# Routing weights packed by token parity: spreads on 64 rows of the array, bias on 128 rows

## What is computed

```
a = layer_norm(channel_norm(x)) * w + b
left  = mask * (a @ Wl + bl) * sigmoid(a @ Gl + gl);  right likewise
t[i,j,c] = sum_k left[i,k,c] * right[j,k,c]              # one 256x256x256 product per channel
x = x + (layer_norm(t) @ Wo + bo) * sigmoid(a @ Wg + bg)
y = layer_norm(x)
p = softmax(y @ Wr + br)                                  # 8 experts
top-2 of p, renormalised to g1 + g2 = 1
x = x + sum over the 2 picked experts e of g_e * (y @ We[e] + be[e])
```

## Time and profile before

| | |
|---|---|
| median of 3 runs | 1189.2 us (1185.09 to 1192.96) |
| profiled execution | 1190.0 us, of it the span in the profile 1188.0 us |
| PE busy | 1080.7 us (91%) |
| PEld busy | 594.6 us (50%) |
| DVE busy | 882.2 us (74%) |
| POOL busy | 747.6 us (63%) |
| ACT busy | 598.8 us (50%) |

### The profile page before, as it was taken

One profiled execution on the slowest core, in us unless ns is written; L12 is line 12 of the kernel. 1 busy time (PEld: TensorE's weight loads), 2 busy tenths in 40 slices (PEclk: granted clock), 3 DMA queues, 4 the chain that ended last, 5 costly groups with the idle time before them and its releaser, 6 DMA issues.

```text
span 1188.0 us, 21300 instructions
## 1 busy us (share of the span) xinstructions
PE 1080.7 (91%) x5402; PEld 594.6 (50%) x5402; DVE 882.2 (74%) x3030; ACT 598.8 (50%) x1070; POOL 747.6 (63%) x728
## 2 busy tenths in 40 slices
PE   1788989889786599999999999999999999999987
PEld 1566666678674344444444444444444444454432
DVE  3999999611115768888888888887888788888872
ACT  0455666411111245666566556565656565656552
POOL 5777888121222357777777767776767776777632
PEclk9899999899887879999999999999999999999986
DMA  7388679967770101111111111111111111111100
GB/s 194 115 268 284 229 274 293 328 198 235 209 234 27 30 19 51 46 45 42 50 47 44 36 54 40 49 45 45 36 53 36 54 36 53 36 54 36 36 27 27
DMA packets 98895, 119.15 MB, mean 100 GB/s; under 512 B 6390, under 2 KB 72182, under 8 KB 96758
## 3 DMA queue, kind: packets, MB, share of 16 engines
q1 hardware_dynamic: 97138, 117.74, 30.9%
q10 hardware_dynamic: 1668, 0.46, 0.2%
HBM read 67.33 MB, written 50.33 MB: 99 GB/s over the span
## 4 chain that ended last, share of the span: by engine, by line
PE 75%; DVE 14%; issue 5%; DMA 2%; ACTq 1%; POOL 1%; ACT 1%; SPq 1%; DVEq 0%; POOLq 0%
PE b_m L807 22%; PE ring L793 9%; PE ein L710 7%; DVE stage L889 6%; PE b_d L754 6%; PE b_g L746 6%; PE b_t L747 5%; PE pr_a L672 4%; PE b_m L801 3%; DVE bst L876 3%; PE b_g L741 3%; PE b_g L735 3%; PE ring L815 3%; PE b_t L735 2%; PE ring L822 1%
## 5 line engine op out<-in xcount | busy, mean ns | idle before, releaser
L451 POOL TENSOR_TENSOR zb<-bcs,x2d 128x512 f32<-128x512 f32 x224 | 285.7, 1275 | 234.8 <-ACT bcs L588 233.6
L807 PE MATMUL b_m<-zb,w_exp 128*64 128x512 f32 x1024 | 284.7, 636 | 0.1
L1052 DVE TENSOR_TENSOR zb<-ring,x2d 128x512 f32<-128x512 f32 x288 | 197.5, 686 | 90.9 <-PE ring L793 90.2
L588 ACT ACTIVATE bcs<-ring 128x512 f32<-128x512 f32 x224 | 133.9, 598 | 245.5 <-PE ring L793 245.2
L572 ACT ACTIVATE x2d<-x2t 64x512 f32<-64x512 f32 x256 | 160.5, 627 | 3.4
L672 PE MATMUL pr_a<-w_proj,xts 64*128 64x256 f32 x1024 | 138.3, 399 | 22.1 <-DVE stage L889 21.4
L889 DVE SCALAR_TENSOR_TENSOR stage<-pr_a,mt,sig_a 128x128 f32<-128x128 f32 x512 | 147.8, 418 | 9.4 <-ACT sig_a L521 9.4
L793 PEld LDWEIGHTS ring<-wt,sel 32*128 32x128 f32 x512 | 49.4, 186 | 177.6 <-DVE zb L1052 83.1
L793 PE MATMUL ring<-wt,sel 32*128 32x512 f32 x512 | 131.0, 504 | 5.2 <-DVE zb L1052 4.4
L672 PEld LDWEIGHTS pr_a<-w_proj,xts 64*128 64x128 f32 x1024 | 95.1, 189 | 51.0 <-issue 30.9
L521 ACT ACTIVATE sig_a<-pr_a 128x512 f32<-128x512 f32 x128 | 76.4, 597 | 78.9 <-PE pr_a L672 78.9
(11 more groups left out here) (133 smaller groups left out, 1820.7 us busy)
## 6 DMA issues: line engine op xcount, KB each, us to landing
left_right_scratch<-stage SPq DMA_DIRECT2D x16, 2048.0 KB, 7.5
chunk<-left_right_scratch SPq DMA_DIRECT2D x24, 1024.0 KB, 9.0
xc<-in_x SPq DMA_DIRECT2D x64, 256.0 KB, 2.7
out<-outc SPq DMA_DIRECT2D x64, 256.0 KB, 2.0
chunk<-left_right_scratch SPq DMA_DIRECT2D x12, 384.0 KB, 7.5
chunk<-left_right_scratch SPq DMA_DIRECT2D x8, 192.0 KB, 4.9
chunk<-left_right_scratch SPq DMA_DIRECT2D x4, 256.0 KB, 8.0
chunk<-left_right_scratch SPq DMA_DIRECT2D x8, 64.0 KB, 4.7
```

What stands on the lines that cost most here:

```text
L451: pool.tensor_tensor(zb[:, m % NZ, :], bcs[:, tiles_before(POOL_TILES, ku, ku, m) % 2, :], x2d[:, ku % 2, m % 2, :], ALU.mult)\
L588: act.activation(bcs[:, tiles_before(POOL_TILES, ku, ku, m) % 2, :], ring[:, bcast_bank(ku % 2, m), :], ACT.Copy).then_inc(bcast_out, 1)
L807: ins = pe.matmul(b_m[t * C:(t + 1) * C, :], w_exp[:, ep, :], zb[:, (2 * ep + t) % NZ, :], start=False, stop=ep == EP - 1, skip_group_chec ...
L1052: dve.tensor_tensor(zb[:, m % NZ, :], ring[:, bcast_bank(ku % 2, m), :], x2d[:, ku % 2, m % 2, :], ALU.mult)\
```

## The change

- In a step, the token order becomes `(j t h)`: on the 128 rows of one transpose, rows 0 to 63 now hold the tokens of parity 0, the even unit's on the first 32 and the odd unit's on the second 32, and rows 64 to 127 those of parity 1. It is made by the two VectorE instructions that put the logits and the variances into that order.
- A spread of parity `m % 2` now reads the 64 rows `64*(m%2)` onward. Since those rows hold both units, `sel` has a second form (`sel[:, w]`, `w` the unit's parity) whose rows of the other unit are zero.
- The bias matmuls now read all 128 rows, with `bias_hi` and `bias_lo` in two forms in the same way.
- Set-up: `eb_wide`, `bias_hi`, `bias_lo` and `sel` are twice as wide; GpSimd makes `sel` with two instructions of 128x512, and one of 128x16 and a wait are gone.

```diff
-            ("sel", [P, E, C], F32R), ("kind", [P, 4, E]),
+            ("sel", [P, 2, E, C], F32R), ("kind", [P, 4, E]),
...
-                    sp.dma_start(eb_wide[row:row + E, t % 2 * C:t % 2 * C + C], expert_b).then_inc(const_in, 16)
+                    sp.dma_start(eb_wide[row:row + E, t % 2, t // 2 * C:t // 2 * C + C], expert_b).then_inc(const_in, 16)
...
-            pool.tensor_tensor(kind[:, 0:2, :], kind[:, 0:2, :], kind[:, 2:4, :], ALU.add).then_inc(sel_made, 1)
-            pool.wait_ge(sel_made, 2)
-            ins = pool.tensor_tensor(sel[:, :, :], kind[:, 0, :].unsqueeze(2).broadcast_to([P, E, C]),
-                                     kind[:, 1, :].unsqueeze(2).broadcast_to([P, E, C]), ALU.add)
+            for w in range(2):
+                ins = pool.tensor_tensor(sel[:, w, :, :], kind[:, w, :].unsqueeze(2).broadcast_to([P, E, C]),
+                                         kind[:, 2 + w, :].unsqueeze(2).broadcast_to([P, E, C]), ALU.add)
...
-                rows = slice(ku % 2 * 2 * ROUTE + m % 2 * ROUTE, ku % 2 * 2 * ROUTE + m % 2 * ROUTE + ROUTE)
-                pe.matmul(ring[:, bcast_bank(ku % 2, m), :], sel[rows, m // 2 * 2:m // 2 * 2 + 2, :].rearrange("p e c -> p (e c)"),
+                rows = slice(m % 2 * 2 * ROUTE, (m % 2 + 1) * 2 * ROUTE)
+                pe.matmul(ring[:, bcast_bank(ku % 2, m), :], sel[rows, ku % 2, m // 2 * 2:m // 2 * 2 + 2, :].rearrange("p e c -> p (e c)"),
                           wt[rows, ku // 2 % 2, :], start=True, stop=True).then_inc(bcast_ready, 1)
...
-                rows = slice(ku % 2 * 2 * ROUTE, (ku % 2 + 1) * 2 * ROUTE)
                 for part, b in enumerate((bias_hi, bias_lo)):
-                    pe.matmul(b_m[:, :], b[rows, :], wt[rows, ku // 2 % 2, :], start=part == 0, stop=False, skip_group_check=True)
+                    pe.matmul(b_m[:, :], b[:, ku % 2, :], wt[:, ku // 2 % 2, :], start=part == 0, stop=False, skip_group_check=True)
...
-            dve.tensor_copy(bias_hi[:, :], eb_wide[:, :]).then_inc(set_step, 1)
+            dve.tensor_copy(bias_hi[:, :, :], eb_wide[:, :, :]).then_inc(set_step, 1)
...
-                            ins = dve.tensor_scalar(v32[:, 0:TOK].rearrange("p (j h t) -> p h j t", h=2, t=2), x_stat[:, :, :, 2].rearrange("p (h j) t -> p h j t", h=2), 1.0 / C, EPS_LN, ALU.mult, ALU.add)
+                            ins = dve.tensor_scalar(v32[:, 0:TOK].rearrange("p (j t h) -> p h j t", h=2, t=2), x_stat[:, :, :, 2].rearrange("p (h j) t -> p h j t", h=2), 1.0 / C, EPS_LN, ALU.mult, ALU.add)
...
-                dve.tensor_copy(lg[:, b, :, :].rearrange("p (z j h t) e -> p z j h (t e)", z=2, j=2, h=2)[:, :, :, h, :],
-                                logits).then_inc(back_done, 1)
+                dve.tensor_copy(lg[:, b, :, :].rearrange("p (z j t h) e -> p z j t h e", z=2, j=2, h=2)[:, :, :, :, h, :],
+                                logits.rearrange("p z j (t e) -> p z j t e", t=2)).then_inc(back_done, 1)
```

More of the change, by code:

```diff
@@ L127, in metaformer_kernel @@
         w_og = keep("w_og", [P, 2, P])
-        bias_hi = keep("bias_hi", [P, P], F32R)
-        bias_lo = keep("bias_lo", [P, P], F32R)
+        bias_hi = keep("bias_hi", [P, 2, P], F32R)
+        bias_lo = keep("bias_lo", [P, 2, P], F32R)
         router_bias = keep("router_bias", [P, E])
@@ L147, in metaformer_kernel @@
             ("w_nat", [C, 6, 2, C]), ("ln_col", [P, 4]), ("bias_row", [1, 6 * C]), ("w_diff", [P, 6 * C]),
-            ("ones", [P, P]), ("e_nat", [P, E, C]), ("r_nat", [P, E]), ("eb_wide", [P, P]),
+            ("ones", [P, P]), ("e_nat", [P, E, C]), ("r_nat", [P, E]), ("eb_wide", [P, 2, P]),
             ("mask_in", [P, 2, N])])
-        setup_bytes = 4 * (12 * C + 4 + 6 * C + 6 * C + P + E * C + E + P + 2 * N)
+        setup_bytes = 4 * (12 * C + 4 + 6 * C + 6 * C + P + E * C + E + 2 * P + 2 * N)
         (xts, _, w_proj, mt, r_all, b_all, xa, xs, sig_a, stage, bst, nv, nh, ny, nt) = layer([
@@ L329, in _ @@
             pool.memset(w_router, 0.0).then_inc(pool_const, 1)
-            pool.memset(eb_wide[:, :], 0.0).then_inc(pool_const, 1)
+            pool.memset(eb_wide[:, :, :], 0.0).then_inc(pool_const, 1)
             pool.memset(w_og[:, :, :], 0.0).then_inc(pool_const, 1)
@@ L790, in bcast @@
                     if isinstance(u, int) and u == 0:
-                        pe.wait_ge(sel_made, 3)
-                rows = slice(ku % 2 * 2 * ROUTE + m % 2 * ROUTE, ku % 2 * 2 * ROUTE + m % 2 * ROUTE + ROUTE)
-                pe.matmul(ring[:, bcast_bank(ku % 2, m), :], sel[rows, m // 2 * 2:m // 2 * 2 + 2, :].rearrange("p e c -> p (e c)"),
+                        pe.wait_ge(sel_made, 2)
+                rows = slice(m % 2 * 2 * ROUTE, (m % 2 + 1) * 2 * ROUTE)
+                pe.matmul(ring[:, bcast_bank(ku % 2, m), :], sel[rows, ku % 2, m // 2 * 2:m // 2 * 2 + 2, :].rearrange("p e c -> p (e c)"),
                           wt[rows, ku // 2 % 2, :], start=True, stop=True).then_inc(bcast_ready, 1)
@@ L929, in _ @@
                 dve.tensor_tensor(w_router[part, half * E:half * E + E], r_nat[part, :], ps_set[part, 7, 0:E], ALU.subtract)
-            dve.tensor_copy(bias_hi[:, :], eb_wide[:, :]).then_inc(set_step, 1)
+            dve.tensor_copy(bias_hi[:, :, :], eb_wide[:, :, :]).then_inc(set_step, 1)
             dve.wait_ge(set_step, 2)
-            dve.tensor_tensor(bias_lo[:, :], eb_wide[:, :], bias_hi[:, :].bitcast(F32), ALU.subtract).then_inc(set_dve, 1)
+            dve.tensor_tensor(bias_lo[:, :, :], eb_wide[:, :, :], bias_hi[:, :, :].bitcast(F32), ALU.subtract).then_inc(set_dve, 1)
             with dve.Fori(0, CHUNKS) as c:
```

## The result

The changed kernel takes 1169.86 us (median of 3 runs, 1169.37 to 1174.58) against 1189.2: 19.3 us less, and the ratio of the means of the runs is 0.985 with a 95% interval of 0.9818 to 0.9883. That is faster by over 1%, which had a chance of 0.39. The direction was right; of the size, the forecast had 11 of the 19 us. The profiled execution took 1169.4 us (span 1167.4), to be held against 1190.0 before.

What follows compares the result with a forecast made beforehand. TensorE's own list was taken to bound the unit stage. From 1190.0 us, 12.3 came off for the bias pair and 0.3 was added for copies and the narrow gap, giving 1178.0 us, range 1171 to 1189.

Steps and rivals of the forecast that it cites:

- What bounds the kernel: Unit stage: TensorE's own list is the time, busy 696.57 of 705.00 us, as long as VectorE keeps up.
- The opening cost after a change of shape: Bias pair behind transposes: no shape change on 128 rows saves 0.215 us in 57 units, 12.3 us less.
- an fp32r record is one run, 0.213 us: Bias pair: two runs of 512 columns take 0.43 us, leaving 0.23 of its 0.66 for the shape change.
- Spreads on 64 rows at no cost: 256 spread pairs on 64-row halves run side by side as before: 0, with ends of 0 and 1.0 us more.
- The halves overlap: Spread pairs; judges the slower rival that 64-row fp32r matmuls don't run side by side: 1233 us, chance 0.06.
- VectorE's cover: VectorE copies cost 0, covered by 62.3 us of waits for spreads; smallest typical gap 0.30 us falls to 0.08.
- Set-up: Before the unit stage: extra GpSimd work is hidden behind 6.06 us of idle time until TensorE's transposes.
- the slack of 0.4: Set-up: VectorE's bias split may grow by some 0.4 us before TensorE's products; any excess costs at most 0.5 us.
- The clock: Start of the unit stage: granted clock falls to 0.51, counted only as run spread, 4 us either way.
- the gain did not stay away: Bias pair; judges the rival that its gain stays away or is halved: 1184 or 1190 us, chance 0.22.
- VectorE did not become the bound: Unit stage; judges the rival that VectorE eats a third to half of the gain: 1182 to 1184, chance 0.10.
- they aren't cheaper to switch to than blocks of 32 rows: Spread pairs; judges the rival that halves save 0.05 to 0.1 us per pair: 1150 to 1165, chance 0.04.

Runs made afterwards that it cites:

- kernel 10: The changed kernel with the bias matmul pair issued twice (hi, lo, hi, lo), so the output holds the biases twice: 1213.69 us against 1168.63 for the changed kernel.
- kernel 4: The changed kernel with spreads 0 to 3 on 128 rows as well: 1166.12 us, ratio 0.9782 to the kernel before.
- kernel 2: The changed kernel with spreads back on 32 rows, bias still on 128 rows: 1171.96 us, ratio 0.9832 to the kernel before.
- kernel 8: The kernel before (old token order) with the bias and spreads 0 to 3 on 128 rows: 1165.66 us, ratio 0.978; measured again later, 1167.92 us.
- kernel 1: The kernel before (old token order, 32-row spreads) with the bias alone on 128 rows: 1169.94 us, ratio 0.9824.
- Kernel 6: The kernel before with the bias of the last four units alone on 128 rows: 1185.64 us against 1193.41, ratio 0.994.
- kernel 9: The kernel before, unchanged, run once more for a second trace: 1194.93 us in one run.
- kernel 11: The changed kernel, unaltered, measured again on the third chip: 1168.63 us, ratio 0.9793 to the kernel before.
- kernel 3: The kernel before with both spreads of a pair on the same 64 rows, those of their unit: 1245.56 us, ratio 1.0456.
- kernel 5: The kernel before with the bias alone on 128 rows, except the last four units' bias on 64 rows: 1172.56 us, ratio 0.9821 to the kernel before.
- kernel 7: The kernel before with the bias alone on 128 rows, except units 0 and 1, whose bias stays on 64 rows: 1175.87 us, ratio 0.9855.

## Why the prediction was half right

- **What bounds the kernel**: right. TensorE's list is the time in the steady stretch, and what was cut from it came off the period nearly in full (0.18 of 0.19 us), though TensorE's waits grew by about 2 us over the stage.
- **The opening cost after a change of shape**: right in kind and place. The pair went to 0.47 us, experts and transposes kept their lengths. The size was off: I took 0.215 us for each unit, measured are 0.18 to 0.19. The step at fault is "an fp32r record is one run, 0.213 us": kernel 10 gives 0.235. With that, the 0.66 of before are 2 x 0.235 + 0.19, and 0.19 agrees with the 0.20 between L746 and L747, the row that I had averaged away. In the steady stretch it made 9.6 us, where I had 12.3. The Trainium skill says in "TensorEngine Tiling (Array Packing)", section Tiling Modes, that a change of mode drains the engine. The traces agree in kind: the change of shape costs 0.19 us here, and kernel 4 takes 0.20 off L755 by leaving one out. What share of it is a drain and what share a weight load that nothing covers, no run here shows.
- **Spreads on 64 rows at no cost**: right (491 against 490 ns; kernels 2 and 8). The halves overlap as the 32-row blocks did.
- **VectorE's cover**: right, by a small margin. Its wait fell by 10 us and TensorE's grew by 2. The logits' copy went from 207 to 210 ns on the mean, and kernel 1, in the old order, has 213: the order costs nothing.
- **Set-up**: hidden, as predicted: `sel` on GpSimd takes 2.04 us at 388.7 us, behind which GpSimd is idle for 5.36 us until TensorE's transposes. The split of the biases on VectorE grew by 1.2 us (from 1.08 to 2.31), more than the slack of 0.4 that I had counted; but GpSimd was later in this trace too, and TensorE again started the products on its wait for it (L401), 0.4 us behind the split's end.
- **The clock**: this is what was missing. I saw the lower level at the start of the stage, took its length as a matter of chance, 4 us either way, and did not look at the last units, where the same table would have shown 0.72. It was worth 5.1 us at the start and 10.3 at the end. This is the step that failed: the sum has no term for the clock, on the ground that it only shifts a little from run to run. Kernel 6 shows that the rows of eight bias matmuls bring most of the 10.3 us at the end. At the start it is likely but not clear of chance.
- **The rivals**: the gain did not stay away; that transposes ahead of a product in one shape cost nothing of their own is now shown by kernel 10, since 0.47 is two times 0.235 with nothing left. The rule of the Trainium skill cited from "TensorE: Matmul & The Clock Gate", section Part 3: Packing small matmuls, that a weight load overlaps only on other rows, does not hold here: in the changed kernel a weight load of `bias_lo` takes 0.19 us and the pair, both on all 128 rows, takes 0.47 us in all, so the load is covered but for some 0.02 us. VectorE did not become the bound. The halves overlap, and they aren't cheaper to switch to than blocks of 32 rows (a pair takes 0.42 to 0.43 us with either).

So of the 25 us between kernels 9 and 11, 9.3 are the opening cost that was forecast, and 15.4 came by the clock, at the two ends of the stage. In the first pair of traces the clock's share was the same, but the kernel before had begun its stage 4.4 us early. That the time still came out within about a microsecond of the range is partly luck: the opening cost taken too high (12.3 us for 9.6) and, as far as one trace tells, that early start made up for a part of what the sum left out.

## What to carry to other kernels

Count the changes of array shape in TensorE's list, not the array's use: the bias pair, which needs only 64 rows but stands behind 128-row transposes, was 0.19 us cheaper on 128 rows with zeros. A pair that can run side by side on different rows gains 0.23 us by it (kernel 3); only with 128-row neighbours on both sides was a wide pair as good or slightly better (kernels 4 and 8). And read the granted clock of the first and last stretches of a stage before calling a matmul's width free: where TensorE has gaps, wider matmuls may raise its level.

## What the runs showed of the hardware

- With 64-row bias matmuls in the last four units the granted clock fell to its lower level there in all four traces that have them (before, again before, both spreads on one half, kernel 5), for 27.3, 27.3, 20.4 and 13.6 us ahead of the last 4; with 128-row ones it was lower there for 3.4 us or less in all ten. Save in kernel 3, the work and the waits around them were the same up to the fall. Only the number of rows in use differed, half of them multiplied by zeros. The times of whole runs bear this out in kernel 6 and not in kernel 5.
- The 3.4 us stand in all four traces with a 128-row bias and all spreads on 32 rows (kernels 1, 2, 6, 7), and in one of the six with wider spreads (kernel 10). So the spreads' rows may count a little too; that was not tested by itself.
- At the start of the stage the lower level lasted 17.1 to 20.5 us in the four traces with a 64-row bias throughout that part, 13.7 us in kernel 7, and 6.8 to 10.2 us in the nine with a 128-row one.
- An fp32r matmul of 512 columns follows another on the same rows after 0.235 us at 2.4 GHz (kernel 10), where 512 columns are 0.213; a record of a float32 one of the same width takes 0.43 (L747), two times 0.213 to the hundredth.
- What the clock's behaviour at the loop's restarts depends on is open: it fell there in kernels 7 and 10 and not in the others.
